# A convolution chain on one core: conv1's output as two maxima, with its matmul reading tokens at a stride of 128

## The reference

```python
qkv = xn @ w_qkv + b_qkv                      # xn: x after a batch norm
...                                           # q, k: centred, squared, normalised
kv = jnp.einsum('bnc,bnd->bcd', k2, v)
t2 = jnp.einsum('bnc,bcd->bnd', q2, kv) / math.sqrt(N)
attn = (v + t2) @ w_ln + b_ln
y = jnp.concatenate([attn.reshape(b, h, w, C), shortcut], axis=-1)
y = jax.nn.leaky_relu(_conv(y, w1, 'VALID') + b1, 0.2)   # conv1, 1x1: 96 -> 96
y = jax.nn.leaky_relu(_conv(y, w2, 'SAME') + b2, 0.2)    # conv2, 3x3: 96 -> 96
y = _conv(y, w3, 'VALID') + b3                           # w3, 1x1: 96 -> 48
return y + shortcut
```

## Time and profile before

| What | Value |
|---|---|
| Median of 3 runs | 1320.14 us |
| The profiled execution | 1316.4 us, of which 1314.6 us are its span |
| PE busy | 1194.1 us (91%) |
| DVE busy | 874.0 us (66%) |
| ACT busy | 537.0 us (41%) |
| POOL busy | 150.9 us (11%) |
| Mean granted TensorE clock | 0.95 of full speed |
| DMA queue q1 | 75.73 MB, 41.3% of 16 engines |

### The profile page before, as it was taken

The page is one execution under the profiler, slowest core; times in us unless marked ns, Lnnn a source line. Parts: engine busy times, 40 slices in busy tenths (PEclk is TensorE's granted clock), DMA queues, the critical chain, the costliest instruction groups (busy, mean ns, idle before and its releaser), DMA issues.

```text
span 1314.6 us, 14707 instructions
## 1 busy us (share of the span) xinstructions
PE 1194.1 (91%) x4981; PEld 767.6 (58%) x4981; DVE 874.0 (66%) x1090; ACT 537.0 (41%) x876; POOL 150.9 (11%) x72
## 2 busy tenths in 40 slices
PE   3799888999899998999899998999899998999995
PEld 2565565657565675656566574656656574655533
DVE  5542469954698269965598358974699458982760
ACT  2411435334722545235632446335542447233431
POOL 0400023000400014000400004000310004000000
PEclk9789869999999998999989998999989998999997
DMA  3201710099103960089202980069301980049106
GB/s 61 45 14 29 96 29 0 1 118 133 33 0 41 137 105 0 0 101 134 47 0 37 121 125 0 0 80 141 61 0 19 126 123 14 0 64 129 42 17 89
DMA packets 200077, 76.07 MB, mean 58 GB/s; under 512 B 191245, under 2 KB 191858, under 8 KB 200050
## 3 DMA queue, kind: packets, MB, share of 16 engines
q1 hardware_dynamic: 200050, 75.73, 41.3%
HBM read 13.65 MB, written 6.29 MB: 15 GB/s over the span
## 4 chain that ended last, share of the span: by engine, by line
PE 54%; issue 18%; POOL 8%; SPq 8%; DVE 4%; ACT 3%; DMA 3%; POOLq 0%; DVEq 0%; ACTq 0%
PE bank L1080 33%; POOL y_parts L958 7%; PE bank L1104 4%; PE bank L1091 3%; SPq L832 3%; SPq L857 3%; PE bank L1022 3%; PE bank L1148 2%; DMA y_parts<-a_parts 2%; PE bank L1171 2%; PE bank L1170 2%; POOL tok L953 2%; SPq L853 1%; PE bank L1107 1%; PE bank L1106 1%
## 5 line engine op out<-in xcount | busy, mean ns | idle before, releaser
L1080 PE MATMUL bank<-y_parts,w_h 96*96 96x512 f32 x1152 | 313.6, 423 | 4.6 <-ACT y_parts L1310 4.6
L629 DVE SCALAR_TENSOR_TENSOR dwa<-h1a,dyn,dwa 128x1024 f32<-128x1024 f32 x240 | 294.3, 1274 | 0.0
L1080 PEld LDWEIGHTS bank<-y_parts,w_h 96*96 96x96 f32 x1152 | 192.8, 168 | 108.3 <-issue 14.5
L629 DVE SCALAR_TENSOR_TENSOR dwb<-h1b,dyn,dwb 128x1024 f32<-128x1024 f32 x128 | 155.8, 1275 | 0.0
L1080 PE MATMUL bank<-y_parts,w_l 96*96 96x512 f32 x576 | 154.9, 415 | 0.0
L958 POOL TENSOR_TENSOR y_parts<-y,y_parts 96x512 fp32r<-96x512 f32 x56 | 127.6, 2299 | 193.1 <-ACT y_parts L1310 193.0
L1104 PE MATMUL bank<-a_parts,wt_h 128*96 128x512 f32 x384 | 119.5, 420 | 15.0 <-DMA y_parts<-a_parts 15.0
L1080 PEld LDWEIGHTS bank<-y_parts,w_l 96*96 96x96 f32 x576 | 98.7, 171 | 47.9 <-issue 0.3
L953 POOL TENSOR_TENSOR tok<-tok,u 128x1536 f32<-128x1536 f32 x8 | 22.4, 2798 | 763.3 <-DVE u L570 763.3
L667 DVE SCALAR_TENSOR_TENSOR y<-y 96x512 f32<-96x512 f32 x64 | 90.1, 1408 | 26.9 <-ACT y L1296 25.9
L708 DVE SCALAR_TENSOR_TENSOR a_parts<-v,a_parts 96x512 fp32r<-96x512 f32 x64 | 44.0, 687 | 85.8 <-ACT a_parts L1359 83.0
(11 more groups left out here) (223 smaller groups left out, 1718.2 us busy)
## 6 DMA issues: line engine op xcount, KB each, us to landing
y_parts<-a_parts SPq DMA_DIRECT2D x32, 396.0 KB, 6.1
y_parts<-a_parts SPq DMA_DIRECT2D x64, 192.0 KB, 6.6
a_parts<-a_parts SPq DMA_DIRECT2D x32, 264.0 KB, 3.3
dwa<-in_x_dram SPq DMA_DIRECT2D x64, 96.0 KB, 2.9
tok<-in_x_dram SPq DMA_DIRECT2D x64, 96.0 KB, 4.2
x_even<-y_parts SPq DMA_DIRECT2D x16, 384.0 KB, 8.6
x_odd<-y_parts SPq DMA_DIRECT2D x16, 384.0 KB, 7.9
out_dram<-dwb SPq DMA_DIRECT2D x32, 192.0 KB, 2.3
```

The source lines that it names most:

```text
L629: nc.vector.scalar_tensor_tensor(out=dst, in0=tap_input(n, t), scalar=weight, in1=dst, op0=ALU.mult, op1=ALU.add).then_inc(tap_step, 1)
L1080: last = nc.tensor.matmul(bank[0:C2, :], wgt[:, t, :], src[:, rows, cols], start=t + n == 0, stop=t == TAPS - 1 and n == 2)
```

## The change

conv1's matmul now reads `xq` at a stride of 128, in the order (pair, quarter, block): its bank, and `y1` with it, hold the pixels in order, runs of 16 of a row, and every later instruction reads them one after another. ACT takes the bank out once, multiplied by 0.2 (`conv1_slope`), and its instruction for `y1_h` is gone. DVE does two maxima in place of one instruction: max(bank, 0.2 bank) straight into `y1_h`, and the same into `y1`. The bank is free after the second of them, not after ACT's copy. POOL's low part waits for both.

With it, `xa` goes: x is loaded once into `tok` and its even rows a second time into the place of q in the odd half (12 transfers for each image), which `transpose_x` reads. `load_x` moves to the start of SP's iteration. The table of depthwise steps has none in the conv1 stage and four more around the projection, where the order of the small DVE instructions changes too.

```diff
-        steps_at = (0, 1, 1, 1, 0, 1, 0, 0) + (8, 5, 5, 5, 5, 4, 4, 4) + (1, 1, 1, 3)
+        steps_at = (0,) * CHUNKS + (8, 5, 5, 5, 5, 4, 4, 4) + (2, 1, 3, 4)
...
-            return columns(y1[:, :, :], (k % Y1_BUFFERS) * BANK, [[WQ, PAIRS], [1, WQ], [128, 4]])
+            return columns(y1[:, :, :], (k % Y1_BUFFERS) * BANK, [[RUN, PAIRS], [4, WQ], [1, 4]])
+
+        def bank_tokens(bank):
+            return columns(bank, 0, [[RUN, PAIRS], [4, WQ], [1, 4]])
...
-                    dve.wait_ge(y1_linear, CHUNKS * image + k)
-                    buffer = (k - 1) % Y1_BUFFERS
-                    nc.vector.scalar_tensor_tensor(out=y1[:, buffer, :], in0=y1[:, buffer, :], scalar=SLOPE,
-                                                   in1=y1[:, buffer, :], op0=ALU.mult, op1=ALU.max).then_inc(y1_max, 1)
+                    dve.wait_ge(y1_slope, CHUNKS * image + k)
+                    bank, buffer = ring_c.bank(C_1 + k - 1)[0:C2, :], (k - 1) % Y1_BUFFERS
+                    nc.vector.tensor_tensor(y1_view(y1_h, k - 1), bank_tokens(bank), y1_tokens(k - 1), ALU.max).then_inc(y1h_ready, 1)
+                    nc.vector.tensor_tensor(y1[:, buffer, :], bank, y1[:, buffer, :], ALU.max).then_inc(y1_max, 1)
...
-                        nc.tensor.matmul(bank[0:C2, :], w1_cur[:, :], xq[:, (k - 1) % 2, :], start=True, stop=True)\
+                        nc.tensor.matmul(bank[0:C2, :], w1_cur[:, :], columns(xq[:, :, :], (k - 1) % 2 * BANK, [[WQ, PAIRS], [1, WQ], [128, 4]]),
+                                         start=True, stop=True)\
...
-                        nc.scalar.activation(y1[:, (k - 1) % Y1_BUFFERS, :], ring_c.bank(C_1 + k - 1)[0:C2, :], ACT.Copy)\
-                            .then_inc(y1_linear, 1)
-                    if image is not None and k > 1:
-                        y1_high_part(image, k - 2)
+                        nc.scalar.activation(y1[:, (k - 1) % Y1_BUFFERS, :], ring_c.bank(C_1 + k - 1)[0:C2, :], ACT.Copy, scale=SLOPE)\
+                            .then_inc(y1_slope, 1)
...
+            for q in range(WQ):
+                sp.dma_start(tok[q::WQ, 1, :, Q_AT:Q_AT + C], src[0, q]).then_inc(x_loaded, 16)
```

More of the change, by code:

```diff
@@ L60 @@
 B_COPIES, WT_COPIES, X2_COPIES = 7, 16, 4
+X_LOADS = 3 * WQ
 Y1_BUFFERS = 3
@@ L268, in conv_chain_kernel @@
         C_1, C_2 = 0, 8
-        ring_c = Ring(banks[4:6], [(y1_linear, CHUNKS, n + 1) for n in range(CHUNKS)]
+        ring_c = Ring(banks[4:6], [(y1_max, CHUNKS, n + 1) for n in range(CHUNKS)]
                       + [(y2_ready, CHUNKS, n + 1) for n in range(CHUNKS)])
@@ L766, in iteration @@
                 depthwise_at(back, BY_PROJECT)
+                w3_out(f, PCHUNKS - 1)
+                depthwise_at(back, BY_PROJECT + 1)
+                l1_low_part(f, PCHUNKS - 1)
                 if back is not None:
                     l3_low_part(back, 0)
[L769 to L773, removed]
+                    depthwise_at(back, BY_PROJECT + 2)
                     l3_low_part(back, 1)
@@ L823, in x_rows @@
             return a["x"][image].rearrange("(j b) (q i) c -> b q j i c", b=2, q=WQ)
[L825 to L832, removed]
         def load_x(sp, image):
@@ L918, in iteration @@
             def iteration(f, attn, back):
+                if attn is not None:
+                    load_x(sp, attn)
                 beside_l1(sp, f)
-                if attn is not None and back is not None:
-                    load_xa(sp, attn, PCHUNKS * (f - 1) + 2)
                 if back is not None:
                     beside_l3(sp, back, f + 1)
-                if attn is not None:
-                    load_x(sp, attn)
                 copy_x2(sp, f)
@@ L1028, in attention_sums @@
                 bank = ring_a.take(pe, image, A_G)
-                pe.wait_ge(x_loaded, 32 * WQ * (image + 1))
                 pe.wait_ge(k_scaled, image + 1)
@@ L1295, in conv1_high @@
                             after(act, y1l_last, image)
-                        nc.scalar.activation(y1[:, (k - 1) % Y1_BUFFERS, :], ring_c.bank(C_1 + k - 1)[0:C2, :], ACT.Copy)\
-                            .then_inc(y1_linear, 1)
-                    if image is not None and k > 1:
-                        y1_high_part(image, k - 2)
-                    for i, n in enumerate(expand_beside[k] if f is not None else ()):
+                        nc.scalar.activation(y1[:, (k - 1) % Y1_BUFFERS, :], ring_c.bank(C_1 + k - 1)[0:C2, :], ACT.Copy, scale=SLOPE)\
+                            .then_inc(y1_slope, 1)
+                    for n in expand_beside[k] if f is not None else ():
                         if n >= 4:
                             h1a_rows(f, n)
-                        if k == CHUNKS and i == 0 and image is not None:
-                            y1_high_part(image, CHUNKS - 1)
-                if f is None:
-                    y1_high_part(image, CHUNKS - 1)
-            def y1_high_part(image, k):
-                act.wait_ge(y1_max, CHUNKS * image + k + 1)
-                nc.scalar.activation(y1_view(y1_h, k), y1_tokens(k), ACT.Copy).then_inc(y1h_ready, 1)
             def first_tap(image, n):
```

23 lines of the change are left out of this document (10 added, 13 removed).

## The result

The changed kernel takes 1302.89 us (median of 4 runs, 1302.48 to 1305.95), the one before 1319.99 on the same chip (4 runs, 1317.56 to 1320.87). The ratio is 0.9885, with a 95% interval of 0.9862 to 0.9908: 17 us faster, where 72 were forecast. The profiled execution has a span of 1300.9 us against 1314.6.

The account below looks back on a forecast made before the run. ACT was taken to pace the conv1 stage ahead of conv2, at 2.56 us a chunk. Terms -47.6 - 20.4 + 5 - 8.2 + 2.7 - 3.8 = -72.3 us gave 1248 us, own range 1236 to 1265, with rivals 1236 to 1306.

Parts of the forecast that it names:

- The stride on PE: conv1's matmul reading xq at a stride of 128: no added cost, bounds 0 and 1.04 us a chunk.
- Rival 1: conv1 on PE: the stride costs PE what it cost ACT, +1.04 us a chunk, 1306 us; chance 0.16.
- The conv1 stage: Ahead of conv2: PE sets the pace at 1.78 us a chunk, conv2 starts 6.8 us earlier, seven times, -47.6 us.
- The clock: conv2's first 81 matmuls: PE's pauses stay about 1 us, full clock is kept, -20.4 us on seven bursts.
- DVE and POOL: conv1 stage: maxima 0.74 to 1.26 us, POOL's low part 0.93 to 2.0, blocking at nothing; +5 us taken of 13.
- rival 4: conv1 stage: POOL holds off DVE's maxima too, 3.1 us a chunk, slower, 1330 us; chance 0.05.
- conv2 at full clock: conv2: y2 of bank 1 is ready 1 us before PE wants it; cost 0, bounds 0 to 3 us an image.
- Rival 3: conv2: DVE cannot follow at full clock, two to three us an image given back, about 1266 us; chance 0.08.
- 2: Before conv2: the clock falls all the same as PE pauses, the 20.4 us are not won, 1268 us; chance 0.06.
- 5: conv1 stage: the pace is not ACT's, ACT merely follows POOL, some 3 us a stage won, 1280 us; chance 0.06.
- The projection: After conv2: four more DVE steps, 4.8 us, fit before PE arrives; cost 0, bounds 0 and 1 us an image.
- The loads of x: Transposes of x: the 1.37 us wait goes in six images, -8.2 us; prologue's first transposes wait longer, +2.7.

Follow-up runs that it names:

- the probe: The kernel before with runs of matmuls, transposes and ACT copies at several strides added at its end: float32 matmul records 0.429 us in order, 0.900 in steps of 4.

## Why the prediction was wrong, point by point

**The stride on PE, taken as 0 between bounds of 0 and 1.04 us a chunk, is the step that failed.** It is 0.87 us a chunk, 47 us in all. I chose "PE's own row", the weight loads at a stride of 16, over ACT's 0.52. The row is right and says nothing of the moving operand: the probe's weights in steps of 16 go at 0.10 to 0.11 us once the clock is up, and its float32 moving columns take double the time from steps of 4 on. I had also called the rates near each other, 0.89 ns a column for weights and 0.84 for conv1. The first is of weights and the second of a read in order; what the moving operand gives at a stride no row of before shows. ACT's row was the nearer one: the same size and the same pattern, read from SBUF, only by another engine. Rival 1, at 0.16, came in: it gave 1306 us, 2.82 us a chunk and two records at 2.4 us in the sum with an expand group; measured were 1302.9, 2.65, and 2.21 from conv1's start to the next transposes. The sentence of the Trainium skill beside it (Advanced Engine Details and Errata, SBUF Cachelines) was borne out for float32 moving columns (1042 ns a record against 615), not for weights.

**The conv1 stage** was right apart from that: with the reordering moved to ACT's read, 18.18 - 12.24 = 5.9 us a stage, 42 over seven, against 47.6 less the 5 of risk.

**The clock** was right in size: seven bursts of together 155.5 us before (the prediction's 154.5 is a slip of the pen, its 20.4 is not) take 135.4, which is 20.1 less. The reason that I gave, a pause of PE under 1 us, agrees with the trace (0.41), but no experiment isolates it. What I didn't see is that 5.9 of the 20.1 come with the loads of x alone (149.6 us for the same seven bursts), and by what path stays open.

**DVE and POOL**: the first maximum takes 0.72, so the runs of 4 cost nothing there; the second 0.67; POOL's low part 1.36, between my 0.93 and 1.70. POOL doesn't hold off the maxima, and rival 4 is wrong; that it would hold off an instruction with two inputs in SBUF was right, and showed where I put steps beside conv1.

**conv2 at full clock** was right: 19.35 us, and no wait for `y2` at the third bank in the images of the loop. Rival 3 is out, and so are 2 and 5.

**The projection, taken as 0 with a bound of 1 us an image,** is the second failure: 1.44 us, over the bound. From conv2's end, at 562.57, ACT has the unit ready at 580.8, after 18.2 us: just the 17.1 and 1.1 of my sum. But PE is there at 579.36, after 16.8 and not 18 to 18.6: I had given layer 1's two groups "near 9 at most", and they took 7.7. The order of before with six steps there removes it, for 6 us.

**The loads of x**: the 8.2 us were right (the waits at L1010 added up to 8.8 and are gone), and so was the prologue's price, 15.85 to 18.25, +2.4 for +2.7. The prologue's other term, -3.8, was lost to the stride with the rest: image 0's conv2 starts at 70.76 where it started at 69.67. With ACT reading the bank it starts at 67.80, so about -4 of it came.

With these two steps at their measured size the sum becomes -72.3 + 47 + 7 x 1.44 = -15, and the medians say -17.

## What to carry to other kernels

When a slow access is moved to another engine, price it by the same operand (moving, not weights), the same element type and the same memory, and not by the same engine; if no row shows that, keep the price of the engine that does it now as the expected one. The cheapest home for a reordering is the side of an instruction that lies in PSUM: here it was free for ACT's read and PE's write, and cost 0.43 us a record (PE) or 0.52 (ACT) in SBUF. And a step that is moved out of one stage needs its place in the next one's queue checked, behind each wait there, for 8 us lay in the order and the places of eight steps alone.
